# A fused cross-attention and feed-forward kernel: one copy in two goes from ScalarE to VectorE, one normalised tile in four from VectorE to GpSimd

## The reference, cut to what matters

```python
def _prob(x):
    x = jnp.tanh(x) * 0.499 + 0.5
    return jnp.clip(x / (jnp.sum(x, axis=-1, keepdims=True) + EPS), EPS)

def xattn(q, k, v):                       # q = layernorm(x), k = v = ctx
    q_prob, k_prob = _prob(q), _prob(k)
    log_ratio = jnp.log(q_prob) - jnp.log(k_prob)
    sid = jnp.einsum('bnd,bmd->bnm', q_prob - k_prob, log_ratio)
    attn = jax.nn.softmax(-sid / D ** 0.5, axis=-1)
    f_diff = (v - jnp.einsum('bnm,bmd->bnd', attn, v)) @ W_diff.T + b_diff + q
    h = _layernorm(f_diff, ln_g, ln_b)
    out = jax.nn.gelu(h @ W1.T + b1, approximate=False) @ W2.T + b2 + f_diff
    return _layernorm(out, ln_g, ln_b)

x = x + xattn(_layernorm(x), ctx, ctx)
x = x + fp8_linear(_layernorm(x), Wf, bf)
```

## Time and profile before

| | |
|---|---|
| median of 3 runs | 263.16 us (262.43 to 263.87) |
| the profiled execution | 263.24 us, of which the span from first to last instruction is 261.4 us |
| busy over the span | PE 211.9 us (81%), DVE 221.8 (85%), ACT 215.9 (83%), POOL 187.1 (72%) |
| mean granted TensorE clock | 0.918 of full speed |

### The profile page before, as it was taken

How to read it: one execution, slowest core, us unless ns; L and a number is a source line. 1 busy time by engine, 2 the same in 40 slices (tenths; PEclk the granted TensorE clock), 3 DMA queues, 4 the chain that set the end, 5 groups by cost and what they waited for, 6 DMA issues and landing times.

```text
span 261.4 us, 5919 instructions
## 1 busy us (share of the span) xinstructions
PE 211.9 (81%) x1723; PEld 181.6 (69%) x1723; DVE 221.8 (85%) x843; ACT 215.9 (83%) x772; POOL 187.1 (72%) x248
## 2 busy tenths in 40 slices
PE   2767696854596769988999999999999999999522
PEld 1756585543484658766699998899999899988410
DVE  1999999989879778999833789999999999898995
ACT  4599999998889999997667888889888887777532
POOL 2477766764898879996828386969698787667572
PEclk9997888895579989999999999999999999999955
DMA  5677544530000000000333338897988888988696
GB/s 144 190 216 194 163 140 145 156 98 1 1 0 3 0 3 3 3 3 3 40 43 45 35 43 104 98 134 117 125 133 116 125 128 127 136 120 120 103 161 142
DMA packets 51888, 23.92 MB, mean 91 GB/s; under 512 B 9872, under 2 KB 51728, under 8 KB 51856
## 3 DMA queue, kind: packets, MB, share of 16 engines
q0 software_dynamic: 16384, 8.13, 28.2%
q1 hardware_dynamic: 35040, 15.21, 21.9%
q10 hardware_dynamic: 432, 0.20, 0.3%
HBM read 9.37 MB, written 4.19 MB: 52 GB/s over the span
## 4 chain that ended last, share of the span: by engine, by line
PE 49%; ACT 23%; DVE 20%; issue 4%; DMA 3%; SPq 0%; ACTq 0%; DVEq 0%
PE bank L976 21%; ACT TQK L503 6%; ACT TQK L487 6%; PE bank L967 6%; PE bank L968 5%; PE bank L969 5%; DVE F L801 3%; DVE q_c L778 3%; DVE LN_c L786 3%; ACT PV L498 3%; DMA LN_c<-in_ctx_dram 3%; PE bank L957 2%; ACT vT_c L492 2%; PE bank L994 2%; ACT TQK L530 2%
## 5 line engine op out<-in xcount | busy, mean ns | idle before, releaser
L976 PE MATMUL bank<-W2T,TQK 128*128 128x128 f32 x512 | 68.2, 279 | 0.8 <-ACT TQK L525 0.4
L976 PEld LDWEIGHTS bank<-W2T,TQK 128*128 128x128 f32 x512 | 64.5, 191 | 5.4 <-issue 1.0
L525 ACT ACTIVATE TQK<-bank,b1c 128x512 f32<-128x512 f32 (+1 forms) x68 | 44.5, 661 | 14.9 <-PE bank L969 14.3
L360 POOL TENSOR_TENSOR xrstd<-xvar,pow_c 128x4 f32<-128x4 f32 x16 | 16.8, 1052 | 21.4 <-DVE xvar L694 21.4
L967 PE MATMUL bank<-hTh,W1h 128*128 128x512 f32 (+1 forms) x68 | 30.1, 442 | 0.8 <-DVE hTl L769 0.6
L405 POOL DMA_DIRECT2D F<-rows x17 | 24.7, 1451 | 2.2 <-DVE E_c L764 2.2
L925 PE MATMUL bank<-WdT,vT_c 128*128 128x128 f32 x128 | 22.7, 333 | 4.4 <-ACT vT_c L492 4.4
L968 PE MATMUL bank<-hTl,W1h 128*128 128x512 f32 (+1 forms) x68 | 26.1, 383 | 0.0
L969 PE MATMUL bank<-hTh,W1l 128*128 128x512 f32 (+1 forms) x68 | 25.9, 381 | 0.0
L455 POOL TENSOR_TENSOR xrstd<-xvar,pow_c 128x4 f32<-128x4 f32 (+1 forms) x17 | 24.7, 1454 | 0.4 <-DVE xvar L694 0.4
L925 PEld LDWEIGHTS bank<-WdT,vT_c 128*128 128x128 f32 x128 | 20.2, 240 | 6.5 <-ACT vT_c L492 6.5
(11 more groups left out here) (129 smaller groups left out, 663.3 us busy)
## 6 DMA issues: line engine op xcount, KB each, us to landing
F<-rows POOLq DMA_DIRECT2D x30, 256.0 KB, 4.6
LN_c<-in_ctx_dram SPq DMA_DIRECT2D x16, 256.0 KB, 2.9
X<-in_x_dram SPq DMA_DIRECT2D x16, 256.0 KB, 3.3
out_dram<-F SPq DMA_DIRECT2D x15, 256.0 KB, 3.9
LN_c<-in_L_xattn_W_dram SPq DMA_DIRECT2D x1, 256.0 KB, 4.1
lT_c<-in_L_xattn_W_dram SPq DMA_DIRECT2D x1, 256.0 KB, 3.7
F<-rows POOLq DMA_DIRECT2D x2, 128.0 KB, 4.5
out_dram<-F SPq DMA_DIRECT2D x2, 128.0 KB, 2.3
```

Source lines behind the costliest of these rows:

```text
L525: act.activation(hid(m, j), m1_bank(m, j), ACT.Gelu, bias=b1c[:, j:j + 1]).then_inc(gelu_ready, 1)
L976: last = pe.matmul(M2_B[m.buf][:, i * D:(i + 1) * D], hid(m, j)[:, i * D:(i + 1) * D], W2T[:, j * D:(j + 1) * D], start=(j == 0 and i == 0 ...
```

## The change

ACT's copy L492 stays for even chunks only. For odd chunks (`buf == 1`) DVE copies the transposed context, between the four BATCH_NORM_STATS2 and the addition L727. DVE normalises three tiles of a chunk; the fourth is done by GpSimd, behind the power L360 and ahead of the bias addition L366. Two new semaphores carry this: `vT_dve` (the odd copies) and `q_pool` (GpSimd's tiles). ACT's tanh of q, DVE's statistics of two chunks later (they overwrite the mean that GpSimd reads) and GpSimd's own addition wait for `q_pool`; PE waits for `vT_dve` or `vT_sb` by parity.

```diff
@@ gpsimd, phase1
                     pool.tensor_tensor(buf(xrstd, k, G), buf(xvar, k, G), pow_c[:, 0:k.g], ALU.pow).then_inc(x_rstd, 1)
+                    pool.wait_ge(x_rstd, k.n + 1)
+                    i = G - 1
+                    m = (k.buf * G + i) * 2
+                    pool.tensor_scalar(all_tile(F, k, i), all_tile(X, k, i), xmv[:, m:m + 1],
+                                       xrstd[:, k.buf * G + i:k.buf * G + i + 1],
+                                       ALU.subtract, ALU.mult).then_inc(q_pool, 1)
                 k = at(1)
                 if k.live:
                     pool.wait_ge(q_ready, k.n + 1)
+                    pool.wait_ge(q_pool, k.n + 1)
@@ scalar, phase1
                     last.then_inc(tanh_k, 1)
+                if k.live and k.buf == 0:
                     act.wait_ge(vT_ps, k.n + 1)
                     wait(act, P_ps, k.n - 1)
-                    act.activation(buf(vT_c, k), VT_B[k.buf][:, 0:k.g * D], ACT.Copy).then_inc(vT_sb, 1)
+                    act.activation(buf(vT_c, k), VT_B[0][:, :], ACT.Copy).then_inc(vT_sb, 1)
...
                     act.wait_ge(q_ready, k.n + 1)
+                    act.wait_ge(q_pool, k.n + 1)
@@ vector, phase1
                     last.then_inc(x_bn, 1)
+                if s.live and s.buf == 1:
+                    dve.wait_ge(vT_ps, s.n + 1)
+                    wait(dve, P_ps, s.n - 1)
+                    dve.tensor_copy(buf(vT_c, s), VT_B[1][:, :]).then_inc(vT_dve, 1)
...
                     wait(dve, q_ready, s.n - 1)
+                    wait(dve, q_pool, s.n - 1)
...
-                    for i in range(q.g):
+                    for i in range(G - 1):
@@ tensor, phase1
-                    wait(pe, vT_sb, k.n - 1)
+                    wait(pe, vT_dve if k.buf else vT_sb, k.n // 2)
...
-                    pe.wait_ge(vT_sb, k.n + 1)
+                    pe.wait_ge(vT_dve if k.buf else vT_sb, k.n // 2 + 1)
```

More of the change, by code:

```diff
@@ L269, in xattn_ffn_kernel @@
         vT_ps, vT_sb, P_ps, P_sb = sem("vT_ps"), sem("vT_sb"), sem("P_ps"), sem("P_sb")
+        q_pool, vT_dve = sem("q_pool"), sem("vT_dve")
         norm_step, halfk_ready, norms, lratio = sem("norm_step"), sem("halfk_ready"), sem("norms"), sem("lratio")
```

## The result

| | before | after |
|---|---|---|
| median | 263.12 us (262.43 to 263.87, 4 runs) | 271.46 us (271.26 to 271.82, 4 runs) |
| ratio to before | | 1.0322, 95% interval 1.0298 to 1.0347 |
| profiled execution / span | 263.24 / 261.4 us | 271.26 / 269.4 us |
| busy DVE, ACT, POOL | 221.8, 215.9, 187.1 us | 232.4, 213.3, 199.6 us |
| mean granted TensorE clock | 0.918 | 0.907 |

It went the way that was forecast, and more than twice as far: 8.3 us instead of 3.8, outside the range (263.4 to 270.0).

What follows compares the result with a forecast made beforehand. ACT was taken to bound the first phase at 3.30 us a step, DVE close behind at 3.10. After the change, 14 rings of 3.56 us put L703 3.8 us later: 263.24 + 3.8 = 267.0 us, range 263.4 to 270.0.

Steps and rivals of the forecast that it cites:

- the ring: First phase, from one `xvar` to the next: GpSimd's power, tile and addition, then DVE's statistics; 3.56 us in every step.
- the hold: DVE's L679, reading two SBUF operands, waits for GpSimd's addition L366 to end, at 3.07 us after `xvar`.
- rival A: First phase: L366 does not hold L679, DVE sets the pace with its own work; 2.4 us less, 260.8; chance 0.16.
- What bounds the phase before: First phase: ACT never rests at 3.30 us a step; DVE 3.10, GpSimd 2.3.
- The copy on DVE, 0.59 us, and its wait for PE at nothing: Odd steps of the first phase: copying from PSUM costs DVE's queue 0.59 us, PE's transpose comes well before.
- The price of GpSimd's tile: GpSimd's new first-phase TENSOR_SCALAR tile: 0.44 us as for L378, of which the queue sees 0.43.
- The other end kept, 0.64: Upper price for GpSimd's new tile, from L394, the dearest one-tile form: 0.64 us.
- rival B: GpSimd's tile takes 0.64 us, making each first-phase step 3.75; 2.7 us more, 269.7; chance 0.10.
- The sum: Chunk 1's `xvar` at 11.34, chunk 15's at 61.65, L703 at 65.2 against 61.44: 3.8 us later, 267.0 us.
- The last tiles held too: End of first phase: chunk 15's tiles on DVE wait for GpSimd's addition; the first ends at 64.81.
- What follows moves with it: Everything behind L703, where the first phase hands over, moves with it; 3.8 us later, second phase untouched.
- Rival C: First phase: tile costs GpSimd's queue 0.26 us, or L679 is let go earlier; step 3.39, 264.6 us; chance 0.10.

Runs made afterwards that it cites:

- tile_last: Changed kernel with GpSimd's order turned: power, bias addition of the chunk before, then the tile; 263.66 us, ratio 1.0029.
- few_copies: Kernel before with DVE copying the transposed context of chunks 4, 8 and 12 alone, nothing new on GpSimd; 261.88 us, ratio 0.9963.
- no_add: Changed kernel without GpSimd's bias addition, copy and tile kept; 260.35 us, ratio 0.9911.
- half_add: Changed kernel with GpSimd's bias addition 256 instead of 512 columns wide; 264.22 us, ratio 1.0051.
- tile_muladd: Changed kernel with multiply and add instead of subtract and multiply in GpSimd's new tile; 266.80 us, ratio 1.0137.
- probes: Kernel before with six one-tile TENSOR_SCALAR instructions more on GpSimd, right behind its constants where it was idle; 263.16 us.

## Why the tile takes 0.80 us

Two explanations were open: what the instruction computes, or where it stands (behind a power, beside DVE's statistics). Two runs tell them apart.

```diff
-                                       ALU.subtract, ALU.mult).then_inc(q_pool, 1)
+                                       ALU.mult, ALU.add).then_inc(q_pool, 1)
```

> The changed kernel with the two operations of GpSimd's new tile replaced: multiply and add instead of subtract and multiply, operands and place the same; every fourth tile of q is so computed wrongly. Theory 1 (the pair of operations sets GpSimd's price, 0.80 us against the 0.44 of L378, which multiplies and adds): the tile takes 0.44, the ring 3.58, the time 271.4 - 14 x 0.34 = 266.7. Theory 2 (the place sets it: behind a power, beside DVE's statistics, or the layout of its operands): tile at 0.80, time 271.4.

Measured: 266.80 us, 1.0137 (1.0093 to 1.0181), and the tile in the same place with the same operands:

```profile
L365 POOL TENSOR_SCALAR F<-X,xmv,xrstd x16: 447/448/453, 10.4 to 63.0; 128x128 f32<-128x128 f32 x16
```

The other run puts six such instructions where GpSimd has nothing else to do:

```diff
+            for n, (o0, o1, two) in enumerate(((ALU.subtract, ALU.mult, True), (ALU.mult, ALU.add, True),
+                                               (ALU.mult, ALU.mult, True), (ALU.add, ALU.add, True),
+                                               (ALU.subtract, ALU.mult, False), (ALU.mult, ALU.add, False))):
+                at_n = (T - 1 - n) * D
+                pool.tensor_scalar(F[:, at_n:at_n + D], ident[:, :], half_c[:, 0:1],
+                                   pow_c[:, 0:1] if two else 0.25, o0, o1)
```

> The kernel before with six one-tile TENSOR_SCALAR instructions more on GpSimd, right behind its constants, where it was idle until 9.3 us; their output is overwritten later. In order: subtract and multiply, multiply and add, multiply twice, add twice, each with two per-partition operands; then subtract and multiply, multiply and add with one such operand and one constant. Theory 1 (operations): the first about 0.80, the second 0.44, apart from all other work. Theory 2 (place): both 0.44. The time is that of before, 263.

Measured: 263.16 us. GpSimd's timeline, in the order of the list:

```profile
2.74 0.80 POOL L360 TENSOR_SCALAR F<-ident,half_c,pow_c 128x128 f32<-128x128 f32 x1
3.54 0.44 POOL L360 TENSOR_SCALAR F<-ident,half_c,pow_c 128x128 f32<-128x128 f32 x1
3.97 0.45 POOL L360 TENSOR_SCALAR F<-ident,half_c,pow_c 128x128 f32<-128x128 f32 x1
4.41 0.81 POOL L360 TENSOR_SCALAR F<-ident,half_c,pow_c 128x128 f32<-128x128 f32 x1
5.21 0.72 POOL L360 TENSOR_SCALAR F<-ident,half_c 128x128 f32<-128x128 f32 x1
5.91 0.36 POOL L360 TENSOR_SCALAR F<-ident,half_c 128x128 f32<-128x128 f32 x1
```

With two operations in the instruction the first decides: 0.80 and 0.81 when it subtracts or adds, 0.44 and 0.45 when it multiplies (multiply-add and multiply-multiply differ in the second alone and cost the same); 0.72 and 0.36 when the second operand is a constant. The starts lie as far apart as these durations, to 0.02. It is neither the place nor DVE, which was idle over the first four. L378, from which the price was taken, multiplies first; normalising as (x - mean) times the inverse deviation subtracts first. Why GpSimd is slower then is not shown by any run, and the rule does not reach to instructions with one operation: in the trace of before L386 only multiplies, by one per-partition operand, and takes 0.61 us in 13 of 15 cases; L394 only adds and takes 0.64.

## Whether the hold costs, and how much

If DVE is held until the addition ends, then a shorter addition must give back what its end moves. First half of it:

```diff
-                    pool.tensor_tensor(tiles(chunk(X, k)), tiles(chunk(X, k)), over_tiles(b_r, k.g),
+                    half = X[:, k.at * D:(k.at + 2) * D]
+                    pool.tensor_tensor(tiles(half), tiles(half), over_tiles(b_r, 2),
                                        ALU.add).then_inc(xb_ready, 1)
```

> The changed kernel with GpSimd's bias addition 256 instead of 512 columns wide: two tiles of each chunk of x are left without ln_b. Theory (the ring: DVE's first small statistics instruction is held until that addition ends): the addition ends 0.24 + 1.06 + 0.08 + 0.77 + 0.72 = 2.87 us after the variance, even steps take 2.87 + 0.03 + 0.46 = 3.36, odd ones DVE's own 3.43, mean 3.40 against 3.92: 14 x 0.52 = 7.3 less, 264.2. DVE's first small instruction is about 0.65 long in even steps, 0.16 in odd ones. Rival (the hold comes from GpSimd's tile, or from any overlap, and does not scale with the addition): 269 or more.

Measured: 264.22 us, 1.0051 (1.0037 to 1.0064), against 264.2 expected. The steps take 3.40 and 3.43, where 3.36 and 3.43 were expected. DVE's L690 in an even and in the next odd step, then GpSimd's addition in the even one:

```profile
47.98 0.72 DVE L690 TENSOR_TENSOR xmv<-xstat 128x8 f32<-128x8 f32 x1
...
51.98 0.16 DVE L690 TENSOR_TENSOR xmv<-xstat 128x8 f32<-128x8 f32 x1
```

```profile
47.94 0.74 POOL L375 TENSOR_TENSOR X<-X,rows 128x256 f32<-128x256 f32 x1
```

Held until 48.70 beside an addition that ends at 48.68; free in the odd step, which the copy makes longer. Then all of it:

```diff
                 k = at(1)
-                if k.live:
-                    pool.wait_ge(q_ready, k.n + 1)
-                    pool.wait_ge(q_pool, k.n + 1)
-                    if is_piece(k, 0):
-                        pool.wait_ge(br_in, 16)
-                    pool.tensor_tensor(tiles(chunk(X, k)), tiles(chunk(X, k)), over_tiles(b_r, k.g),
-                                       ALU.add).then_inc(xb_ready, 1)
-
-            run_steps(chunks, 1, phase1)
+
+            run_steps(chunks, 0, phase1)
+            pool.wait_ge(br_in, 16)
...
-            dve.wait_ge(xb_ready, NC)
```

> The changed kernel without GpSimd's bias addition: x goes on without ln_b. Copy and tile stay as they are, GpSimd's tile ends 0.24 + 1.06 + 0.08 + 0.80 = 2.18 us after the variance, before DVE's statistics come at 2.23. Theory (ring): no hold is left, DVE sets the pace with 2.84 in even and 3.43 in odd steps as rival A of the prediction worked out, 260.8. Rival (DVE's or PE's own waits behind the copy cost a part): over 263.

Measured: 260.35 us, 0.9911 (0.9891 to 0.993), 0.45 below the expectation. DVE runs at its own pace. From one normalisation to the next it takes 2.83 us without a copy between them (46.51 - 43.68) and 3.44 with one (49.95 - 46.51):

```profile
43.68 0.86 DVE L756 TENSOR_SCALAR F<-X,xmv,xrstd 128x128 f32<-128x128 f32 x3
...
46.51 0.86 DVE L756 TENSOR_SCALAR F<-X,xmv,xrstd 128x128 f32<-128x128 f32 x3
...
49.95 0.85 DVE L756 TENSOR_SCALAR F<-X,xmv,xrstd 128x128 f32<-128x128 f32 x3
```

So the expensive tile, the copies and the new waits by themselves are not what makes the change slow: without the addition they run 2.5 us faster than the kernel before. (The addition is real work that this run leaves out; it is a measure of the hold, no version to use. The kernel before without its addition was not run.)

**Another order.** The tile behind the addition instead of ahead of it, so that the addition runs under DVE's statistics of x and its own addition, which read one SBUF operand at most:

```diff
                     pool.tensor_tensor(buf(xrstd, k, G), buf(xvar, k, G), pow_c[:, 0:k.g], ALU.pow).then_inc(x_rstd, 1)
-                    pool.wait_ge(x_rstd, k.n + 1)
-                    i = G - 1
-                    m = (k.buf * G + i) * 2
-                    pool.tensor_scalar(all_tile(F, k, i), all_tile(X, k, i), xmv[:, m:m + 1],
...
                                        ALU.add).then_inc(xb_ready, 1)
+                k = at(0)
+                if k.live:
+                    pool.wait_ge(x_rstd, k.n + 1)
+                    i = G - 1
+                    m = (k.buf * G + i) * 2
+                    pool.tensor_scalar(all_tile(F, k, i), all_tile(X, k, i), xmv[:, m:m + 1],
...
```

> The changed kernel with GpSimd's order turned: power, bias addition of the chunk before, and only then the tile. The addition then ends at 2.55 us after the variance, the tile at 3.33. Theory (any GpSimd instruction that reads whole tiles of SBUF holds DVE's two-operand instructions, the tile too): the statistics are held by the tile instead, ring 3.6 to 3.8, 267 to 270. Rival (only the addition with its two operands holds): even steps 2.57 + 0.46 = 3.03, odd ones 3.43, 262.

Measured: 263.66 us, 1.0029 (1.0015 to 1.0043). Neither expectation: 3.3 us under the one and 1.7 over the other. The even step shows why, DVE and then GpSimd:

```profile
47.29 0.36 DVE L691 TENSOR_TENSOR xmv<-xstat 128x8 f32<-128x8 f32 x1
47.58 0.15 DVE L692 TENSOR_TENSOR xgap<-xstat 128x4 f32<-128x4 f32 x1
47.76 0.31 DVE L698 SCALAR_TENSOR_TENSOR xgap<-xgap 128x4 f32<-128x4 f32 x1
47.99 0.16 DVE L699 TENSOR_SCALAR xmv<-xmv 128x4 f32<-128x4 f32 x1
```

```profile
46.35 1.27 POOL L368 TENSOR_TENSOR X<-X,rows 128x512 f32<-128x512 f32 x1
47.61 0.80 POOL L375 TENSOR_SCALAR F<-X,xmv,xrstd 128x128 f32<-128x128 f32 x1
```

The addition holds L691 to 47.65, as ever. The tile runs from 47.61 to 48.41, but the instruction held beside it, L698, is done at 48.07 and the next two are free: the tile holds for about 0.45 of its 0.80 us. Steps were 3.19 and 3.46. The changed kernel has the same in step 1, where no addition is near: its tile runs from 10.54 to 11.34, and the L689 that starts in it is done at 11.01:

```profile
10.74 0.27 DVE L689 TENSOR_TENSOR xmv<-xstat 128x8 f32<-128x8 f32 x1
```

The obvious guess is that it holds while it reads. If so, the cheap form, which has the same data to read, must hold as long:

```diff
-                                       ALU.subtract, ALU.mult).then_inc(q_pool, 1)
+                                       ALU.mult, ALU.add).then_inc(q_pool, 1)
```

> The run tile_last with multiply and add in GpSimd's tile instead of subtract and multiply, so that one tile of q in four is computed wrongly. It asks how long a one-operand tile holds DVE. Theory 1 (only while it reads, about 0.43 us, the price of the cheap form, whatever it computes): DVE's instructions beside it are as long as in tile_last, 0.31 for the three-operand one in even steps and 0.18 for the first in odd ones, though the tile is 0.44 instead of 0.80. Theory 2 (about half of the tile): the hold shrinks with the tile, to 0.22, and both are at 0.16. Theory 1 gives the time of tile_last, 263.7, since DVE's steps stay.

Measured: 263.35 us (one run), beside 262.54 for the kernel before. GpSimd's tile is 0.44 there, and DVE's instructions in the even step are the same as beside 0.80:

```profile
47.41 0.35 DVE L691 TENSOR_TENSOR xmv<-xstat 128x8 f32<-128x8 f32 x1
...
47.87 0.31 DVE L698 SCALAR_TENSOR_TENSOR xgap<-xgap 128x4 f32<-128x4 f32 x1
```

The tile ends at 48.17 there and L698 at 48.18: the cheap tile holds for all of its length, the dear one for the same 0.45. The hold does not follow the length of the tile. That it is the reading is the explanation that fits, but it is not shown: no run separates reading from the rest of such an instruction. It also fits: the power, 1.05 us long, reads four columns, and holds none of the 64 tiles beside it.

## A version that beats both

What can be had is what DVE has to spare: 3.30 - 3.10 = 0.20 us a step. Three copies fit, with nothing new on GpSimd:

```diff
+        BY_DVE = (4, 8, 12)
...
+                if k.live and k.n not in BY_DVE:
                     act.wait_ge(vT_ps, k.n + 1)
                     wait(act, P_ps, k.n - 1)
...
+                if s.live and s.n in BY_DVE:
+                    dve.wait_ge(vT_ps, s.n + 1)
+                    wait(dve, P_ps, s.n - 1)
+                    dve.tensor_copy(buf(vT_c, s), VT_B[s.buf][:, :]).then_inc(vT_dve, 1)
```

> The kernel before with the transposed context of chunks 4, 8 and 12 alone copied by DVE, all four tiles normalised by DVE, nothing new on GpSimd. Theory: DVE has 0.20 us a step to spare against ACT and lets it catch up; from chunk 0's addition to chunk 13's ACT needs 43.5 - 3 x 0.48 = 42.1, DVE 13 x 3.10 + 3 x 0.59 + 1.18 - 0.79 = 42.5: 1.0 us less than before, 262.0. Rival (a step with a copy throws DVE and GpSimd out of step so that the statistics meet the addition, or ACT waits): no gain, 263.

Measured: 261.88 us against 262.90, 0.9963 (0.9949 to 0.9977): 1.0 us less, the expected number. In its one trace the phase accounts for only half of that: L711, the counterpart of L703, starts at 60.97 instead of 61.44.

```profile
60.97 0.22 DVE L711 TENSOR_SCALAR NORM<-SUM 128x112 f32<-128x112 f32 x1
```

From chunk 0's addition to chunk 13's are 43.10 us, not 42.5; at chunk 8 DVE waited 0.58 for x to be loaded, which the expectation did not have. The other half microsecond lies behind the phase and is not explained. The tile in its better place added to that, as an edit of the kernel with the tile last:

```diff
+        BY_DVE = (4, 8, 12)
...
-                if k.live and k.buf == 0:
+                if k.live and k.n not in BY_DVE:
...
-                if s.live and s.buf == 1:
+                if s.live and s.n in BY_DVE:
```

> The two edits that cost least put together: GpSimd normalises every fourth tile behind its bias addition, and DVE copies the transposed context of chunks 4, 8 and 12 alone. Theory: a step without a copy takes DVE 3.19 us (tile_last), one with a copy 3.46, so DVE needs 13 x 3.19 + 5 x 0.27 - 0.80 = 42.0 from chunk 0's addition to chunk 13's and ACT 42.1, against 43.5 before: 1.4 less, 261.5. Rival (the last chunks' tiles meet GpSimd's queue at the end of the phase, and the steps drift into holds): 262.5 or more.

Measured: 261.65 us against 262.54, 0.9963 (0.9947 to 0.9979), 0.9 us less. The ratio is that of few_copies; the further 0.4 us do not show in the times, whose interval is 0.4 us to either side. In the trace the phase did what was expected: 41.94 us from chunk 0's addition to chunk 13's against 42.0, and L720, the counterpart of L703, starts 1.3 before it.

```profile
60.12 0.21 DVE L720 TENSOR_SCALAR NORM<-SUM 128x112 f32<-128x112 f32 x1
```

Both versions beat the kernel before, by about 0.4%. Which of the two is faster is not shown; the first does it with the smaller edit.

## Why the prediction was right in its way and wrong in its size

- **What bounds the phase before**: right. ACT at 3.30 us a step, DVE at 3.10 with nothing to wait for: in few_copies, where ACT is relieved and DVE not held, the steps with no copy of any kind take 3.09 to 3.10 from step 3 on.
- **The copy on DVE, 0.59 us, and its wait for PE at nothing**: right. In the changed kernel the first instruction behind it starts 48.79 - 48.20 = 0.59 later, and DVE shows no wait for PE.
- **The hold**: right in its place and its rule, from three rows of before. Even and odd steps take the same time, and L689 ends 0.02 to 0.03 behind the addition in both; it is 1.24 and 0.64 long where 0.9 and 0.3 were forecast, because the tile makes the addition late. no_add and half_add give back what the ring says. That a held instruction "did nothing until GpSimd was done" is a little too strong: the one of 0.68 ended 0.55 behind, those of 0.16 end 0.03 behind, so about 0.13 us had passed. The ring used the measured 0.03.
- **The price of GpSimd's tile**: here it failed. The step "The same form (two per-partition operands, out of place) is L378, 0.44" took the form for the shapes and operands, and left the operations out. It measured 0.80, of which the queue sees 48.74 - 47.98 = 0.76 instead of 0.43. The other end kept, 0.64, was also too low, and so was rival B's 269.7. Rows of before could have warned: L386 (0.61, one multiplication) and L394 (0.64, one addition) are dearer than L378 with its two operations and two operands, so neither the shapes nor the number of operands set the price. But no row there subtracts or adds first and then does a second operation, and none is at 0.80. The run tile_muladd puts the cheap operations in, and the whole working comes out: steps of 3.56 to 3.57 against 3.56, chunk 15's `xvar` at 61.57 against 61.65, L713 at 65.17 against 65.24, 266.8 us against 267.0.

```profile
65.17 0.20 DVE L713 TENSOR_SCALAR NORM<-SUM 128x112 f32<-128x112 f32 x1
```

- **The sum**: in the changed kernel L703's counterpart starts at 70.01 where 65.24 was forecast, 4.8 late. The rings are (66.18 - 11.46 - 0.11) / 14 = 3.90 on average (3.92, but 3.59 in step 2) instead of 3.56: 4.8. The start of chunk 1's `xvar`, 11.46 for 11.34, adds 0.1; step 9's copy of weights costs 0.11 to 0.12 in the longer ring instead of 0.47, 0.35 less; the end from chunk 15's `xvar` to L713 is 3.83 for 3.59, 0.2 more.

```profile
11.46 0.17 DVE L704 TENSOR_TENSOR xvar<-xgap,xmv 128x4 f32<-128x4 f32 x1
...
66.18 0.17 DVE L704 TENSOR_TENSOR xvar<-xgap,xmv 128x4 f32<-128x4 f32 x1
...
68.29 1.80 DVE L763 TENSOR_SCALAR F<-X,xmv,xrstd 128x128 f32<-128x128 f32 x3
70.01 0.21 DVE L713 TENSOR_SCALAR NORM<-SUM 128x112 f32<-128x112 f32 x1
```

- **The last tiles held too**: right. L763 of chunk 15 takes 1.80 us for three tiles instead of 0.86, beside GpSimd's addition.
- **What follows moves with it**: nearly. L713 is 8.57 later than L703 was, the profiled execution 8.02 longer; about half a microsecond is given back in the later phases. No effect of the change is shown there: from this instruction to the end the traces of before and all versions take between 199.1 and 200.5 us.
- **Rival B** had the kind of error right, a dear tile, at a price that was still too low. **Rival A** was the right account of what is left without the hold (260.8 against 260.35 in no_add), but the hold is there, so it fell. **Rival C** falls with the tile's 0.80.

## What to carry to other kernels

Before work goes to an engine with time to spare, lay its timeline over that of the engine it shares SBUF with: what counts is where the longer queue makes its long reading instructions end, not its busy share. GpSimd had 1 us a step to spare here, and using it made the kernel slower, since one more instruction pushed its 1.27 us addition into DVE's two-operand statistics. And take an elementwise price on GpSimd only from a row with the same operations in the same order, or measure it in a quiet place first.

## What the runs showed of the hardware

- A GpSimd TENSOR_SCALAR of 128x128 fp32 takes 0.80 to 0.81 us when its first operation adds or subtracts, 0.44 to 0.45 when it multiplies (two per-partition operands); 0.72 and 0.36 with a constant as the second operand (probes). This holds for two operations in one instruction; with one operation and one per-partition operand multiplying takes 0.61 and adding 0.64 (L386, L394 of before).
- An eight-column DVE instruction with two SBUF operands took up to 1.24 us instead of 0.16 beside a GpSimd addition of two SBUF operands, and ended 0.02 to 0.03 us behind it. A DVE TENSOR_SCALAR with constants, four columns wide, took 1.28 in the same way in step 2 of the changed kernel (beside an addition from 13.64 to 14.92). The profile shows both as long instructions, not as waits:

```profile
13.67 1.28 DVE L697 TENSOR_SCALAR xmv<-xmv 128x4 f32<-128x4 f32 x1
```

- The hold need not last for the whole instruction. The Trainium skill (SBUF — State Buffer, Who interferes with whom) has the shared ports locked for all of it; for the addition the trace agrees, for GpSimd's tile (about 0.45 of 0.80 us) and its power (none of 1.05) it does not.
- DVE's copy from PSUM, its BATCH_NORM_STATS2 and its addition with one operand in PSUM took the same time beside GpSimd's reading instructions as before (0.67, 0.86, 0.68 us).
